# Row tiles over 64 slots with one product chunk a slot, shorter GpSimd chains, a second block's heads ahead of the steps, and no filler products

## The chip, the core and the metric

The kernel runs on one core of a Trainium2 chip. Its engines are TensorE (PE in the profile, its weight loads PEld), VectorE (DVE), ScalarE (ACT), GpSimd (POOL) and SyncE (SP), each with an instruction queue of its own, taken in order; they meet through semaphores. The metric is the device time of one execution in microseconds. Before the change the median of 3 runs is 1,875.82 us (1,875.80 to 1,886.55).

## The reference

Input x is 4 x 512 x 256 (batch B, time T, width D), cond is 4 x 256. Two layers follow each other, each added to its input. The first is a transformer block in the Poincare ball, all in fp32; the second is an LSTM with 256 units over the 512 time steps. Cut to what matters:

```
def plin(x, w, b): return expmap0(logmap0(x) @ w + b)      # the maps need the norm of each row
xm = expmap0(layer_norm(logmap0(x)) * (1 + sc_msa) + sh_msa)
q, k, v = heads(plin(xm, w_q, b_q)), ...                   # 16 heads of 16
out_h = expmap0(softmax(qt @ kt.T / 4) @ vt)               # each row attends to all 512
attn_out = plin(from_heads(out_h), w_o, b_o)
x = mobius_add(x, expmap0(g_msa * logmap0(attn_out)))
xm = expmap0(layer_norm(logmap0(x)) * (1 + sc_mlp) + sh_mlp)
ff = plin(plin(xm, w_f1, b_f1), w_f2, b_f2)                # 256 -> 1024 -> 256
x = mobius_add(x, expmap0(g_mlp * logmap0(ff)))            # then x = x_in + this
xW = x @ Wx + b                                            # LSTM, 512 steps, h0 = cond
def step(h, c, xw_t):
    a = xw_t + h @ Wh                                      # 4 x 1024
    i, f, o, g = sigmoid, sigmoid, sigmoid, tanh of its quarters
    c = f * c + i * g;  h = o * tanh(c)
```

A step needs the one before it. The block's rows need the attention of their block of 128 time positions, and row tile n (the 4 batches x 32 time positions 32n to 32n+31) must be through the block before step 32n can start.

## The kernel before

Up to about 254 us the kernel loads, normalizes x and computes q, k, v for 16 row groups, in loops. Then comes one sequence of slots, the same on all engines: slot g runs from FIRST (-126) to 511, and a slot g >= 0 contains step g of the LSTM. `pieces(g, ...)` adds what else stands in the slot, in this order:

- **Heads.** `attention(g)`: 256 heads of attention (4 blocks of 128 positions x 4 batches x 16 heads). `head_slot(n)` says where head n stands: block 0 in slots -126 to -63, one a slot; block 1 in slots 0 to 63; blocks 2 and 3 from slot 64 on, every second slot. A head is 4 score products on TensorE (L575), two exps of 128 x 512 on ScalarE, one in its slot and one in the next (L814, L808), a subtraction in two halves on VectorE (L1060) and, five slots later, 8 products with the values (L587).
- **Merges.** `merged(k, r)`: after 16 heads their norms are put right, over 9 slots, with 13 operations on GpSimd.
- **Row tiles.** `post(n, r)`: the 16 row tiles, each spread over PAUSE = 48 slots r, starting at slot 32n - 48, so that two tiles overlap by 16 slots. r = 0: product with w_o (L620) and its bias as a product (L622); r = 1 to 20: two GpSimd chains for the Moebius addition (`mobius_arg`, `mobius_factors`), then the norm and the scale (`to_ratio`, `to_norm`); r = 24 a transpose; r = 25 to 28 w_f1 (L637), two chunks a slot; r = 29 to 32 w_f2 (L645); r = 30, 31 the norm of the hidden row (L653); r = 34 to 40 Moebius again; r = 41 transpose (L659), r = 42 to 45 w_x, the input part of the gates (L669), two chunks a slot.
- **Output.** The 32 finished steps of a ring are transposed (L711), added and stored.

A *chunk* here is a set of fp32 products that streams 1,024 columns as the kernel's own planner counts them: two products of 128 columns, or one of 256, at four passes.

A **step** is on TensorE 32 products of 8 columns (L693) that add to gate inputs in PSUM; every 16 steps `put_round` loads the next 16 steps' inputs into PSUM first (L683). VectorE sums the halves (L1154, L1156, L1158), ScalarE takes tanh (L906, L908, L910), VectorE makes the cell (L1163), ScalarE its tanh (L912), and VectorE writes the new state in two fp16 halves (L1170, L1172), for which TensorE waits.

At the end of each slot `keep_busy` (L735) issues filler products of 256 columns into unused columns of a bank, onto zeros, until a slot has about 3,000 columns (3,600 where it has many of its own, 1,300 in the head slots ahead of the steps).

GpSimd's chains work on one number a row. In `Chain.link` every operation signals a semaphore and the engine waits for it before the next (L244 is a power, L292 and L294 belong to `clip`). Since each engine's queue is in order, a wait of one piece holds up the steps and heads that stand behind it. PSUM bank pM is shared, in an order that `PM_ORDER` computes and `wait_pM` enforces.

Of the kernel before, what the change touches and what calls it, by code (L numbers as in the profile page):

```python
# [43 lines left out]
class Chain:  # L44
# [23 lines left out]
FIRST = -126  # L68
PAUSE = 48
# [20 lines left out]
PM_READ = {"merged": "m_oc", "rows": "n_n1", "norm": "n_nfc", "out": "o_s"}  # L90
PM_ORDER = [use for slot, rank, use in sorted(
    [(merged_slot(k) + 8, 0, ("merged", k)) for k in range(NT)] +
    [(RING * n - PAUSE, 2, ("rows", n)) for n in range(NT)] +
    [(RING * n - PAUSE + 30, 1, ("norm", n)) for n in range(NT)] +
    [(RING * n + RING + 1, 3, ("out", n)) for n in range(NT)])]
# [17 lines left out]
def bass_hyperbolic_block_then_lstm(nc, x, cond, w_q, b_q, w_k, b_k, w_v, b_v, w_o, b_o, w_f1, b_f1, w_f2, b_f2,  # L113
                                    w_ada, b_ada, w_x, w_h, b_l, out):
    ctx = ExitStack()
    with ctx:
# [237 lines left out]
        def _(pool):  # L354
# [64 lines left out]
            def mobius_arg(ch, p, done):  # L419

                N = lambda name: one(name + p)
                clip(ch, N("s1"), N("n1"), 1, N("ca"), N("cb"))
# [4 lines left out]

            def mobius_factors(ch, p, nsq_x, done):

                N = lambda name: one(name + p)  # L430
# [4 lines left out]
                ch.link(g.tensor_tensor(N("cd"), N("cc"), N("y2"), ALU.add))
                ch.link(g.tensor_tensor(N("ca"), nsq_x, N("y2"), ALU.mult))
                ch.link(g.tensor_tensor(N("cb"), N("ca"), N("cc"), ALU.add))
                ch.link(g.tensor_scalar(N("ca"), N("cb"), EPS, None, ALU.max))
                power(ch, N("den"), N("ca"), DOWN, 1)
                ch.link(g.tensor_tensor(N("al"), N("cd"), N("den"), ALU.mult))  # L440
                ch.link(g.tensor_scalar(N("cb"), nsq_x, -1.0, 1.0, ALU.mult, ALU.add))
                ch.link(g.tensor_tensor(N("cc"), N("cb"), N("fac"), ALU.mult))
                g.tensor_tensor(N("be"), N("cc"), N("den"), ALU.mult).then_inc(s[done], 1)
# [775 lines left out]
```

## Time and profile before

| | before |
|---|---|
| median of 3 runs | 1,875.82 us |
| profiled execution | 1,876.28 us, span 1,874.4 us |
| mean granted clock | 0.858 |
| PE busy | 1,638.3 us (87%), 26,135 matmul records |
| DVE busy | 1,161.2 us (62%) |
| ACT busy | 936.6 us (50%) |
| POOL busy | 552.4 us (29%) |
| chain that ended last | PE 59%, POOL 11%, issue 7%, DVE 6%, ACT 3% |

Busy time is the union of an engine's records. PEclk is the TensorE clock that was granted: 1.0 is 2.4 GHz, 0.5 is 1.2 GHz. An fp32 product is split in the trace into two records. A row of a timeline gives the start in us, the time taken by the group, engine, line, operation, what it writes and reads, how many records it joins, and in brackets the idle time ahead of it and who ended it.

### The profile page before, as it was taken

To read this page: it belongs to the slowest core of one execution; us is meant where nothing else is said; L and a number is where in the kernel's file an instruction comes from. 1 tells how busy PE (TensorE), PEld (TensorE's weight loads), DVE (VectorE), ACT (ScalarE), POOL (GpSimd) and SP (SyncE) were. 2 spreads that over 40 slices of the span, in tenths; PEclk is the share of its full clock that TensorE was granted. 3 is DMA by queue.
4 is the path that set the end of the run, shared out by engine and by line. 5 is a ranking of instruction groups with operands and counts; after the bars stand their busy time and mean duration, and the time that the engine had idled before them with its cause. 6 is when DMAs were issued, how large, how long until landed. Compare 5 with 4: busy or idle time off the path is not lost.

```text
span 1874.4 us, 68150 instructions
## 1 busy us (share of the span) xinstructions
PE 1638.3 (87%) x26135; PEld 1394.2 (74%) x26135; DVE 1161.2 (62%) x6482; ACT 936.6 (50%) x3335; POOL 552.4 (29%) x1726
## 2 busy tenths in 40 slices
PE   3755589634999999999999999999999999999998
PEld 3544457423878888888787888888888888888887
DVE  6455555301677776767677777777766656666665
ACT  0334457412667565656565656565644544444443
POOL 4222212324042433333324242333333131413100
PEclk9676765555678689989899989898989999999999
DMA  7000000000000000000000000000000000000000
GB/s 225 0 0 0 0 1 1 1 0 3 2 3 8 3 9 3 9 3 9 3 9 3 9 5 6 9 3 8 3 8 3 9 2 8 5 3 6 3 6 5
DMA packets 16721, 18.53 MB, mean 10 GB/s; under 512 B 6036, under 2 KB 15384, under 8 KB 16408
## 3 DMA queue, kind: packets, MB, share of 16 engines
q1 hardware_dynamic: 13016, 10.51, 2.0%
q8 instruction: 201, 3.29, 0.7%
q10 hardware_dynamic: 3392, 3.81, 0.7%
q14 instruction: 112, 0.92, 0.2%
HBM read 12.21 MB, written 2.10 MB: 8 GB/s over the span
## 4 chain that ended last, share of the span: by engine, by line
PE 59%; POOL 11%; issue 7%; DVE 6%; ACT 3%; POOLq 1%; ACTq 0%; DVEq 0%
PE psum L735 19%; PE psum L693 17%; PE psum L669 5%; POOL sc L244 4%; PE psum L575 4%; PE psum L637 4%; PE psum L645 3%; PE psum L587 2%; PE psum L683 2%; PE psum L653 1%; DVE gA L1154 1%; PE psum L620 1%; DVE gF L1156 1%; DVE cnew L1163 1%; PE psum L622 1%
## 5 line engine op out<-in xcount | busy, mean ns | idle before, releaser
L735 PE MATMUL psum<-zeros,ident 128*128 128x256 f16 x4064 | 586.8, 290 | 19.8 <-DVE gF L1156 13.7
L693 PEld LDWEIGHTS psum<-hl,wh 128*128 128x128 f16 x16384 | 489.9, 97 | 75.7 <-DVE hl L1172 60.1
L693 PE MATMUL psum<-hl,wh 128*128 128x8 f16 x16384 | 516.4, 172 | 4.6 <-DVE hl L1172 3.3
L735 PEld LDWEIGHTS psum<-zeros,ident 128*128 128x128 f16 x4064 | 385.8, 103 | 113.1 <-DVE gF L1156 38.0
L906 ACT ACTIVATE tA<-gA 128x16 f32<-128x16 f32 x512 | 110.6, 216 | 523.9 <-DVE gA L1154 521.0
L1154 DVE TENSOR_REDUCE gA<-psum 128x16 f32<-128x32 f32 x512 | 96.8, 189 | 231.9 <-PE psum L693 228.9
L1060 DVE TENSOR_TENSOR weights<-w,weights 128x256 f16<-128x256 f32 x512 | 204.0, 419 | 38.5 <-ACT weights L808 38.4
L292 POOL TENSOR_SCALAR sc<-sc 128x1 f32<-128x1 f32 x97 | 23.5, 243 | 691.6 <-DVE sc L1131 299.6
L244 POOL TENSOR_TENSOR sc<-sc,cst 128x1 f32<-128x1 f32 (+1 forms) x260 | 198.3, 763 | 48.1 <-POOL sc L292 18.1
L808 ACT ACTIVATE weights<-psum 128x512 f16<-128x512 f32 x256 | 149.3, 583 | 22.1 <-PE psum L587 21.9
L814 ACT ACTIVATE w<-psum 128x512 f32<-128x512 f32 x256 | 149.9, 586 | 0.8 <-PE psum L575 0.7
L912 ACT ACTIVATE ot<-cnew 128x8 f32<-128x8 f32 x512 | 109.7, 214 | 80.5 <-DVE cnew L1163 24.5
L1170 DVE TENSOR_TENSOR hl<-ot 128x8 f16<-128x8 f32 x512 | 89.8, 175 | 93.0 <-ACT ot L912 92.0
L1163 DVE TENSOR_TENSOR_SCAN cnew<-cmul,cadd 128x24 f32<-128x24 f32 x512 | 107.2, 209 | 29.2 <-DVE cadd L1160 1.7
L575 PE MATMUL psum<-qTs,kT 64*128 64x128 f16 x1024 | 121.9, 252 | 2.5 <-issue 1.9
L1172 DVE TENSOR_TENSOR_SCAN hl<-ot,hl 128x24 f16<-128x24 f32 x512 | 106.6, 208 | 17.9 <-DVE hl L1170 0.2
L908 ACT ACTIVATE cmul<-gF 128x8 f32<-128x8 f32 x512 | 107.6, 210 | 0.0
L910 ACT ACTIVATE tO<-gO 128x8 f32<-128x8 f32 x512 | 105.9, 207 | 0.3
L669 PE MATMUL psum<-place,wx 128*128 128x128 f32 x512 | 99.1, 354 | 3.8 <-ACT arena L897 3.3
L1158 DVE TENSOR_REDUCE gO<-psum 128x8 f32<-128x16 f32 x512 | 88.9, 174 | 17.5
L587 PE MATMUL psum<-vs,weights 128*128 128x33 f16 x2048 | 96.4, 184 | 1.3 <-DVE weights L1060 0.8
L1156 DVE TENSOR_REDUCE gF<-psum 128x8 f32<-128x16 f32 x512 | 88.8, 173 | 8.7
(232 smaller groups left out, 2262.8 us busy)
## 6 DMA issues: line engine op xcount, KB each, us to landing
arena<-in_x_dram SPq DMA_DIRECT2D x4, 512.0 KB, 9.8
wf<-in_L_cond_w_f_dram SPq DMA_DIRECT2D x2, 1024.0 KB, 16.8
xr<-in_x_dram SPq DMA_DIRECT2D x64, 32.0 KB, 1.7
out_dram<-place SPq DMA_DIRECT2D x64, 32.0 KB, 1.6
qTs<-in_L_cond_w_ada_dram ACTq DMA_DIRECT2D x1, 1536.0 KB
oT<-in_L_cond_Wh_dram ACTq DMA_DIRECT2D x1, 1024.0 KB, 14.4
wx<-in_L_cond_Wx_dram SPq DMA_DIRECT2D x1, 1024.0 KB, 18.5
rows<-in_L_cond_b_ada_dram ACTq DMA_DIRECT2D x4, 128.0 KB, 14.2
```

Of the source, the lines that this page charges most:

```text
L244: ch.link(nc.gpsimd.tensor_tensor(dst, src, cst[:, which, 0:w], ALU.pow))
L575: last = mm(bank[m % 2][:, kc * P:(kc + 1) * P], kT[part, b, hp, kc * P:(kc + 1) * P], qTs[part, k, hp, :], start=True, stop=True, skip_gr ...
L587: last = mm(pV[:, h % 8 * W1:(h % 8 + 1) * W1], weights[:, m % 4, wl, kc * P:(kc + 1) * P], vs[:, k % B, kc, h, :], start=kc == 0 and wl = ...
L669: last = mm(pP[:, gi % 4 * P:(gi % 4 + 1) * P], wx[:, kc, c * P:(c + 1) * P], XT[:, kc, :], start=kc == 0, stop=kc == KD - 1, skip_group_c ...
L693: last = mm(cols, wh16[:, half, kc, (g0 + c) * P:(g0 + c + 1) * P], hl[:, :, kc, :, 2].rearrange("p e b -> p b e"), start=False, stop=c == ...
L735: mm(pF[:, D:2 * D], ident16[:], zeros[:], start=False, stop=False, skip_group_check=True)
L808: A(weights[:, m % 4, 0, :], bank[m % 2], ACT.Exp, scale=1.0 / (math.sqrt(HD) * QK_UP * QK_UP)).then_inc(s["t_e"], 1)
L814: A(w32[:, m % 4, :], bank[m % 2], ACT.Exp, scale=1.0 / (math.sqrt(HD) * QK_UP * QK_UP)).then_inc(s["t_E"], 1)
L906: A(tA[:], gA[:], ACT.Tanh, scale=down).then_inc(s["l_tA"], 1)
L1060: d.tensor_tensor(weights[:, m % 4, 1, part], w32[:, m % 4, part], weights[:, m % 4, 0, part], ALU.subtract).then_inc(s["t_l"], 1)
L1154: d.tensor_reduce(gA[:], gate_cols(0, i % ROUND), axis=AX.X, op=ALU.add).then_inc(s["l_gA"], 1)
L1163: d.tensor_tensor_scan(cnew[:].rearrange("p c e -> p (c e)"), cmul[:].rearrange("p c e -> p (c e)"), cadd[:].rearrange("p c e -> p (c e)") ...
```

## The change

- Row tiles take 64 slots instead of 48 (ROW_TILE), and start 65 slots ahead of their step (PAUSE): two tiles overlap by half. Each slot has one chunk of a tile where it had two: w_o in r = 1, 2, w_f1 in eight slots, w_f2 in six, w_x in seven (the last slot has two of its chunks). The bias b_o is added on VectorE instead of by a product.
- w_x uses bank pM, which now passes through one more use in `PM_ORDER`. Gate inputs are stored with time innermost.
- GpSimd's row chains are rewritten: operations with two scalars do the work of two, `Chain.send` issues an operation without waiting for it, and part of the series is computed while other engines work.
- Block 1's heads stand in slots -79 to -16; FIRST is -147. Blocks 2 and 3 start at slots 19 and 147, every second slot. A merge has 13 slots (SETTLE = 12).
- WANTED, EARLY and FIRST_STEPS are 0, and `keep_busy` issues nothing.

The diff, cut:

```diff
-FIRST = -126
-PAUSE = 48
+FIRST = -147
+PAUSE = 65
+ROW_TILE = 64
+SETTLE = 12
-LIGHT, HEAVY, EARLY = 3000, 3600, 1300
+WF1_AT = (26, 27, 28, 29, 30, 31, 33, 34)
+WF2_AT = (35, 36, 37, 42, 42, 43, 43, 44)
+GATES_AT = (57, 58, 59, 60, 61, 62, 63, 63)
+WANTED, EARLY, FIRST_STEPS = 0, 0, 0
-    return (FIRST + i, i, 64 + 2 * i, 192 + 2 * i)[block]
+    return (FIRST + i, FIRST + B * H + 4 + i, 19 + 2 * i, 147 + 2 * i)[block]
...
+    def send(self, ins):
+        self.n += 1
+        ins.then_inc(self.sem, 1)
...
+        def row_scale(ch, done):
+            g = nc.gpsimd
+            ch.send(g.tensor_scalar(one("la"), one("lE"), -2.0, one("z2"), ALU.mult, ALU.add))
+            ch.link(g.tensor_tensor(one("lb"), one("z1"), one("lE"), ALU.add))
+            power(ch, one("lc"), one("lb"), DOWN, 1)
+            ch.link(g.tensor_scalar(one("L1"), one("la"), one("lc"), one("ly"), ALU.mult, ALU.add))
...
-                    mm(pM[:, 0:D], ones[0:1, :], bo[0:1, :], start=False, stop=True, skip_group_check=True).then_inc(s["n_wo"], 1)
+                    d.tensor_tensor(vA, pM[:, 0:D], bo[:], ALU.add).then_inc(s["n_v"], 1)
...
+                for gi in range(GC):
+                    if r == GATES_AT[gi]:
+                        if gi == 0:
+                            pe.wait_ge(s["n_Xc"], n + 1)
+                            wait_pM("gates", n)
+                        else:
+                            pe.wait_ge(s["n_xc"], GC * n + gi)
...
-                wanted = LIGHT if cols < 2048 else HEAVY
-                if t < 0:
-                    wanted = EARLY if t in HEAD_AT else 0
-                count = max(0, -((cols - wanted) // D))
+                if t >= 0:
+                    count = int(min((WANTED - 256 - cols) / D, (1.2 - us) * 2400 / D))
+                    if t < 4:
+                        count = (FIRST_STEPS - 256 - cols) // D
+                else:
+                    count = (EARLY - cols) // D if t in HEAD_AT else 0
```

TensorE in the steps in which w_x's chunks stand, before (L693 is a step's products, L575 scores, L587 weighted values, L669 w_x, L735 fillers):

```order
L693 MATMUL psum<-hl,wh 128x8 x32
L575 MATMUL psum<-qTs,kT 128x128 x4
L669 MATMUL psum<-place,wx 128x128 x4
L735 MATMUL psum<-zeros,ident 128x256 x4
L693 MATMUL psum<-hl,wh 128x8 x32
L587 MATMUL psum<-vs,weights 128x33 x8
L669 MATMUL psum<-place,wx 128x128 x4
L735 MATMUL psum<-zeros,ident 128x256 x5
```

and with the change (L741 a step's products, L620 scores, L632 weighted values, L717 w_x, L685 w_f1 of the next tile):

```order
L741 MATMUL psum<-hl,wh 128x8 x32
L620 MATMUL psum<-qTs,kT 128x128 x4
L717 MATMUL psum<-place,wx 128x128 x2
L685 MATMUL psum<-uT,wf 128x128 x2
L741 MATMUL psum<-hl,wh 128x8 x32
L632 MATMUL psum<-vs,weights 128x33 x8
L717 MATMUL psum<-place,wx 128x128 x4
L685 MATMUL psum<-uT,wf 128x128 x2
```

A step has one chunk of either tile where it had two of one; the last such slot has three; the fillers are gone.

TensorE in the head slots ahead of the steps, before:

```order
L587 MATMUL psum<-vs,weights 128x33 x8
L575 MATMUL psum<-qTs,kT 128x128 x4
L735 MATMUL psum<-zeros,ident 128x256 x3
L587 MATMUL psum<-vs,weights 128x33 x8
L575 MATMUL psum<-qTs,kT 128x128 x4
```

and with the change:

```order
L620 MATMUL psum<-qTs,kT 128x128 x4
L632 MATMUL psum<-vs,weights 128x33 x8
L620 MATMUL psum<-qTs,kT 128x128 x4
L632 MATMUL psum<-vs,weights 128x33 x8
L620 MATMUL psum<-qTs,kT 128x128 x4
```

Only a head's own products are left; 128 heads stand there instead of 64.

GpSimd between the exp of the logarithm and the row scale. Before, the first ten of 29 operations:

```order
L465 TENSOR_TENSOR sc<-sc 128x1
L466 TENSOR_TENSOR sc<-sc 128x1
L244 TENSOR_TENSOR sc<-sc,cst 128x1
L468 TENSOR_TENSOR sc<-sc 128x1
L469 TENSOR_SCALAR sc<-sc 128x1
L470 TENSOR_TENSOR sc<-sc 128x1
L244 TENSOR_TENSOR sc<-sc,cst 128x1
L269 TENSOR_TENSOR sc<-sc 128x1
L270 TENSOR_SCALAR sc<-sc 128x1
L271 TENSOR_TENSOR sc<-sc 128x1
```

and with the change all of them (L256 is a power):

```order
L341 TENSOR_SCALAR sc<-sc 128x1
L342 TENSOR_TENSOR sc<-sc 128x1
L256 TENSOR_TENSOR sc<-sc,cst 128x1
L344 TENSOR_SCALAR sc<-sc 128x1
L345 TENSOR_SCALAR sc<-sc 128x1
L346 TENSOR_TENSOR sc<-sc 128x1
L347 TENSOR_SCALAR sc<-sc 128x1
L348 TENSOR_TENSOR sc<-sc 128x1
L349 TENSOR_SCALAR sc<-sc 128x1
L256 TENSOR_TENSOR sc<-sc,cst 128x1
L351 TENSOR_TENSOR sc<-sc 128x1
```

Eleven are left in this place; ten that need no exp stand ahead of it (L328 to L336).

## Rows read from the trace of the kernel before

**Rows 1.** Page, part 2: granted clock in 40 slices of 46.9 us.
```profile
PEclk9676765555678689989899989898989999999999
```
**Rows 2.** Page, part 5: the fillers; busy us, mean ns, idle before, releaser.
```profile
L735 PE MATMUL psum<-zeros,ident 128*128 128x256 f16 x4064 | 586.8, 290 | 19.8 <-DVE gF L1156 13.7
```
**Rows 3.** Windows, second sum of a step alone: stretch, us, busy (count), PEclk, DMA, GB/s.
```profile
461.80:673.80 212.00, 11.07 (x64) 0.74 0.01 4
673.80:1384.00 710.20, 44.33 (x256) 0.95 0.02 6
1384.00:1757.40 373.40, 25.03 (x144) 0.99 0.02 6
1757.40:1870.00 112.60, 8.38 (x48) 1.00 0.02 4
```
**Rows 4.** Windows of all engines: PE, PEld, DVE, ACT, POOL busy, PEclk, DMA, GB/s.
```profile
276.00:288.00 12.00, 12.00 (x121) 8.69 (x120) 6.51 (x18) 8.91 (x16) 0.21 (x1) 0.50 0.01 1
...
636.00:640.00 4.00, 4.00 (x62) 3.10 (x58) 2.65 (x16) 2.32 (x10) 2.31 (x11) 0.50 0.00 0
```
**Rows 5.** Timeline of a step at granted clock 0.50.
```profile
656.62 1.05 PE L693 MATMUL psum<-hl,wh 128*128 128x8 f16 x32
...
657.27 0.19 DVE L1154 TENSOR_REDUCE gA<-psum 128x16 f32<-128x32 f32 x1 [0.80 <-PE psum L693]
...
657.52 0.39 PE L587 MATMUL psum<-vs,weights 128*128 128x33 f16 x8
...
657.84 0.60 PE L575 MATMUL psum<-qTs,kT 64*128 64x128 f16 x4
...
658.37 2.07 PE L669 MATMUL psum<-place,wx 128*128 128x128 f32 x8
...
658.99 0.76 DVE L1060 TENSOR_TENSOR weights<-w,weights 128x256 f16<-128x256 f32 x2
...
660.24 0.85 PE L735 MATMUL psum<-zeros,ident 128*128 128x256 f16 x3
660.48 0.91 ACT L897 ACTIVATE arena<-psum,blc,unit 128x128 f32<-128x128 f32 x2 [1.05 <-PE psum L669]
...
660.88 0.59 PE L693 MATMUL psum<-hl,wh 128*128 128x8 f16 x15
```
**Rows 6.** Timeline of a step in the tail, granted clock 1.00.
```profile
1841.76 0.21 DVE L1172 TENSOR_TENSOR_SCAN hl<-ot,hl 128x24 f16<-128x24 f32 x1
...
1842.03 1.01 PE L693 MATMUL psum<-hl,wh 128*128 128x8 f16 x32
1842.64 0.19 DVE L1154 TENSOR_REDUCE gA<-psum 128x16 f32<-128x32 f32 x1 [0.53 <-PE psum L693]
```
**Rows 7.** Timeline: ScalarE's exps of heads ahead of the steps.
```profile
273.83 0.60 ACT L808 ACTIVATE weights<-psum 128x512 f16<-128x512 f32 x1 [0.38 <-PE psum L587]
...
274.37 0.60 ACT L814 ACTIVATE w<-psum 128x512 f32<-128x512 f32 x1
...
275.35 0.60 ACT L808 ACTIVATE weights<-psum 128x512 f16<-128x512 f32 x1 [0.38 <-PE psum L587]
```
**Rows 8.** Timeline: TensorE and VectorE wait for a row tile's X.
```profile
544.17 0.48 DVE L1146 SCALAR_TENSOR_TENSOR X<-X,sc,xr 128x256 f32<-128x256 f32 x1 [1.21 <-POOL sc L443]
...
545.23 0.69 PE L659 MATMUL psum<-ident,X 128*128 128x128 f32 x2 [1.23 <-DVE X L1148]
```
**Rows 9.** Timeline: first and last of 29 operations of GpSimd's long chain.
```profile
388.14 0.19 POOL L465 TENSOR_TENSOR sc<-sc 128x1 f32<-128x1 f32 x1 [0.42 <-ACT sc L854]
...
399.96 0.24 POOL L287 TENSOR_SCALAR sc<-mv 128x1 f32<-128x1 f32 x1 [0.20 <-POOL sc L286]
```
**Rows 10.** Timeline: tile 0's first product, step 0's products, the last step's second sum.
```profile
367.04 0.77 PE L620 MATMUL psum<-wo,oT 128*128 128x256 f32 x1 [0.56 <-ACT oT L828]
...
461.02 1.05 PE L693 MATMUL psum<-hl,wh 128*128 128x8 f16 x32
...
1868.53 0.18 DVE L1156 TENSOR_REDUCE gF<-psum 128x8 f32<-128x16 f32 x1
```

More of the change, by code:

```diff
@@ L89 @@
 HEAD_AT = {head_slot(n): n for n in range(HEADS)}
-PM_READ = {"merged": "m_oc", "rows": "n_n1", "norm": "n_nfc", "out": "o_s"}
+PM_READ = {"merged": ("m_oc", 1), "rows": ("n_v", 1), "norm": ("n_nfc", 1), "gates": ("n_xc", GC), "out": ("o_s", 1)}
 PM_ORDER = [use for slot, rank, use in sorted(
[L92 to L95, printed above, removed]
+    [(merged_slot(k) + SETTLE, 0, ("merged", k)) for k in range(NT)] +
+    [(RING * n - PAUSE + 1, 2, ("rows", n)) for n in range(NT)] +
+    [(RING * n - PAUSE + 38, 1, ("norm", n)) for n in range(NT)] +
+    [(RING * n - PAUSE + 57, 1, ("gates", n)) for n in range(NT)] +
+    [(RING * n + RING + 4, 3, ("out", n)) for n in range(NT)])]
 def pieces(g, attention, merged, post, out):
@@ new lines, in row_series @@
+        def row_series(ch):
+            g = nc.gpsimd
+            ch.send(g.tensor_scalar(one("z2"), one("z1"), 2.0, None, ALU.mult))
+            ch.send(g.tensor_tensor(one("ndi"), one("nd1"), cst[:, DOWN, 0:1], ALU.pow))
+            ch.send(g.tensor_scalar(one("negm"), mv1[:, 0:1], -1.0, None, ALU.mult))
+            ch.send(g.tensor_copy(one("varn"), mv1[:, 1:2]))
+            ch.link(g.tensor_tensor(one("nn"), one("nc1"), one("nc1"), ALU.mult))
+            ch.send(g.tensor_scalar(one("small"), one("nn"), SERIES_BELOW, None, ALU.is_lt))
+            ch.link(g.tensor_scalar(one("ser"), one("nn"), 1.0 / 9, 1.0 / 7, ALU.mult, ALU.add))
+            for term in (1.0 / 5, 1.0 / 3, 1.0):
+                ch.link(g.tensor_scalar(one("ser"), one("ser"), one("nn"), term, ALU.mult, ALU.add))
@@ L435, in mobius_factors @@
[L435 to L441, printed above, removed]
@@ L602, in wait_pM @@
                     kind, i = PM_ORDER[before]
-                    pe.wait_ge(s[PM_READ[kind]], i + 1)
+                    read, each = PM_READ[kind]
+                    pe.wait_ge(s[read], each * (i + 1))
             def merged(k, r):
-                if r == 8:
+                if r == SETTLE:
                     pe.wait_ge(s["m_oS"], k + 1)
@@ L629, in post @@
                     last.then_inc(s["n_uT"], 1)
[L630 to L631 removed]
+                if r in WF1_AT:
+                    c = WF1_AT.index(r)
                     pe.wait_ge(s["n_uc"], n + 1)
[L633 to L639 removed]
@@ new lines, in post @@
+                    for kc in range(KD):
+                        last = mm(pP[:, c % 4 * P:(c % 4 + 1) * P], wf1[:, kc, c * P:(c + 1) * P], uT[:, 0, kc, :],
+                                  start=kc == 0, stop=kc == KD - 1, skip_group_check=True)
+                    last.then_inc(s["n_f"], 1)
+                for kc in range(KF):
+                    if r == WF2_AT[kc]:
+                        if kc == 0:
+                            pe.wait_ge(s["n_fc"], KF * n + KF)
+                        last = mm(pP[:, 0:D], fT[:, kc, :], wf2[:, kc, :], start=kc == 0, stop=kc == KF - 1, skip_group_check=True)
+                        if kc == KF - 1:
+                            last.then_inc(s["n_f2"], 1)
```

275 lines of the change are left out of this document (146 added, 129 removed).

## The prediction

> **What bounds the kernel now.** I read the page first. TensorE is busy nearly everywhere, but 587 us of its time are the filler products of L735 [rows 2], so its share says little; the clock it was granted is between 0.5 and 0.7 in much of the first 600 us and near 1.0 later [rows 1]. The count of steps by stretch is more telling: 64 steps in 212 us (3.31 us each), then 256 in 710 us (2.77), 144 in 373 us (2.59), and the last 48 in about 2.33 us each [rows 3]. A step is a loop through three engines: products, sums on VectorE, four tanh on ScalarE, the new state on VectorE, products. In the tail, at the upper clock level (2.4 GHz, granted 1.0), the first sum begins 0.61 us after the first product, and the second half of the state (L1172) begins 0.27 us ahead of the next product; the loop takes 2.33 us there [rows 6]. All that a step takes beyond that is TensorE's other work, or a wait.
>
> Two kinds of excess stand out. Where the clock is granted 0.50 (the lower level, 1.2 GHz [rows 4]), a step with a whole head, two chunks (four fp32 products of 128 columns, which the trace shows as eight records) and three fillers takes 4.26 us (656.62 to 660.88 [rows 5]); nearly all of it is TensorE streaming. And once per row tile TensorE waits for GpSimd's chain of one-column operations: at 545.23 us it had been idle 1.23 us for X, which VectorE could write only after GpSimd [rows 8]. Ahead of step 0 the kernel spends 208 us, from the first head (254 us) to the first step's sum at 461.7 us.
>
> **Prices at the lower clock.** Everything that follows depends on whether TensorE's clock rises without fillers. In the head slots ahead of the steps it ran without a gap for 12 us at a time, with three fillers to a head, and stayed at 0.50; in steps with eight fillers it was at 0.50 too [rows 4]. The change takes away every filler, and its heaviest step streams less than those stretches did. I take 0.50 for the whole recurrence.
>
> The loop itself loses little by that. At 0.50 the 32 products of a step take 1.05 us against 1.01, and the first sum comes 0.65 us after the first product against 0.61 [rows 5, 6]. So a bare step is 2.33 + 0.05 = **2.38 us**. Its bounds are 2.33 (nothing is lost) and 3.31, the mean of the 64 first steps, most of them at 0.50 [rows 3]; I stay near the lower one, since those carried fillers and heads.
>
> Other work starts 0.90 us after the first product (656.62 to 657.52). From start to start [rows 5]: weighted values of a head 0.32, scores 0.53, two chunks (2,048 columns) 1.87. One chunk alone is then 0.94, and I take 1.02, as it changes operands once for half as many columns. A step exceeds 2.38 only if 0.90 plus these does.
>
> **The steps after the change.** Per 32 steps there are 26 chunks (2 for w_o, 8 each for w_f1, w_f2 and w_x), two loads of a round of gates (2,048 columns each) and a few transposes. Two tiles overlap by 32 slots, so chunks pair up: nine steps have two, one has three. With the two rounds that is eleven steps with 1.87 us of large products. With heads, odd steps have scores and even ones weighted values:
> - seven with scores: 0.90 + 0.53 + 1.87 = 3.30, 0.92 over;
> - four with weighted values: 3.09, 0.71 over; together 9.3 us;
> - the triple step 0.90 + 0.32 + 2.73 = 3.95, and 0.64 more because the two w_x chunks of slot 63 stand in one slot and the second waits for ScalarE's copy of the first (0.46 for one of two copies that take 0.91 [rows 5], and 0.18 of handover): 2.2 over;
> - single chunks with a transpose or scores: 1.2 in all;
> - VectorE: its free time in a step is 0.53 us [rows 6]; half a head takes about 0.4 of it (0.76 for two halves) and a row operation 0.48 more [rows 5, 8], so some ten steps that TensorE doesn't stretch are 0.3 to 0.5 longer: 3.7.
>
> Sum 16.4 us per 32 steps. Heads fill steps 19 to 278, 8.1 such rounds: 133 us. Without heads the eleven are 0.39 over, the triple 1.9: 6.3 us per 32, times 6.2: 39 us. The first 19 steps add 2 and the end 0.4. With 512 x 2.38 = 1,219 that makes **1,393 us** between the first and the last sum; before it is 1,406.6 (461.9 to 1,868.5, by the sums of rows 3 and 10). The change gains **13 us** here: it loses about 25 us on bare steps and in the stretches that were at 1.0, wins back some 30 in the first 64 steps, which lose their fillers and one of two exps, and the rest from waits that go.
>
> **GpSimd's chain.** What it removes is real. One row tile's long chain took 29 operations and 12.1 us (388.14 to 400.20 [rows 9]), 0.37 to 0.42 us for a linked operation and 0.75 for a power. Now eleven operations follow the exp (4.7 us by these prices); ten of the rest stand ahead of it, most without waiting for each other. A tile's five chains go from about 35 us to 27. In 64 slots of 2.4 us each stage has one or two slots of its own, so I expect no wait of TensorE for them in the recurrence, and I cost the merge of heads at nothing there: GpSimd is idle over half of each round.
>
> **Ahead of step 0.** Here the slots are short and the cover is gone. One head costs ScalarE two exps 0.54 us apart; TensorE's three fillers made it 1.52 from one to the next [rows 7], now about 1.09. 64 more heads are moved here. Tile 0 may start after 78 heads: 254.4 + 2 + 78 x 1.09 + 3.2 for four merges = 345 us, against 367.0 [rows 10]. Its first 25 slots took 37 us; the chains save 7, a merge on GpSimd now stands in their way (13 of its operations, 9, from the prices above and a wider power), waits of ScalarE and VectorE for results that come later than a 1.09 us slot allows give 2: 41, so 386. Slots 26 to 43 each stream heads and a chunk, 1.87 us mostly: 35, so 421. Then GpSimd has two tiles' chains and a merge in a row: 26, so 447; the eight w_x chunks paired with w_f1's, 14 with their start; the round 1.8. The first product comes at about 463 us, against 461.0: **2 us lost**. Bounds: 445, if the chains hide behind heads, and 480, if each slot's waits add up.
>
> **The sum.** The profiled execution took 1,876.3 us with a span of 1,874.4; the median of the runs is 1,875.8, half a microsecond below. 1,876.3 + 2 - 13.6 = 1,864.7, less 0.5: **1,864 us**.
>
> **Rivals.**
> 1. *The clock stays up.* For it: after the change a bare step leaves TensorE idle only about 1 us at a time. Then a bare step is 2.33, paired chunks fit (0.90 + 0.27 + 0.94 = 2.11), and only the triple step and VectorE's excess are left, 6.3 us a round with heads and 0.8 without: 1,249 us for the steps, 1,720 in all. Against it: 12 us without a gap at 0.50 [rows 4]. 4%. The Trainium skill, "TensorE: Matmul & The Clock Gate", in its table "Why this matters for your kernels", asks only that no long idle gap stand between bursts. By that rule this rival would be the forecast; the gap-free rows at 0.50 show that it isn't enough here.
> 2. *It rises where chunks pair up*, seven slots in a row. The eleven steps lose most of their excess: 61 us with heads, 27 without, 1,776 in all. For it: in the first 64 steps, where two chunks stand in a step, it did rise, to a mean of 0.74 [rows 3]. Against it: those had fillers too. 8%.
> 3. *The part ahead of the steps shrinks*, the chains hiding behind heads: 445, so 1,846. 18%.
> 4. *Slower: the copies reach the tanh.* A chunk now ends with the step, and ScalarE's copy (0.46) starts with the next products; the first tanh follows 0.88 us after them (0.65, and a sum of 0.19 with its handover). By my prices 0.3 us is left. If waking, a second copy and VectorE's row operations together put the tanh 0.2 us late in the 16 to 20 chunk steps, that is 3 to 4 us a round, 50 us over 14 rounds, 1,914 in all; it decides from 0.06 us over all 512 steps, which makes 1,895. For it: at 660.48 ScalarE's copy is still running when the next products start [rows 5]. 22%.
>
> **The numbers.** The forecast's own case has 48% and reaches from 1,845 to 1,888. The range that holds 8 in 10 is 1,825 to 1,905: it leaves out rivals 1 and 2 (12%) and the upper part of rival 4. A measurement of this kernel tells 1% from no change, 19 us: below 1,857 is faster, above 1,895 slower. Faster: 4 + 8 + 16 of rival 3 + 10 of the forecast's case = 38%. Slower: 20 of rival 4 and 2 of the forecast = 22%. The same: 40%.
>
> **What would show it.** The granted clock in the steps: 0.5 nearly throughout, else rival 1 or 2. The last 30 steps: 2.38 us each (2.33 to 2.42). The stretch of steps 64 to 255: about 2.89 us a step; 320 to 463: 2.58. Paired chunks from start to start: 1.87. No wait of TensorE on X or on the normalized rows. First product of step 0 at 445 to 480 us. It is wrong if bare steps exceed 2.45 us, or if a step waits for ScalarE's copies.

## The result, and the profile after

The changed kernel takes **1,778.96 us** (median of 4 runs, 1,772.66 to 1,785.78); before, 4 runs beside them gave 1,875.81. The ratio is 0.9476 (95% interval 0.943 to 0.9522): 5% faster, where 1,864 us had been forecast, with a range that began at 1,825. Ratios leave out executions over 1.5% above the fastest of their kernel and medians keep them, which is why e1 and e4 below look slower by median than by ratio. The profiled execution took 1,775.52 us, its span is 1,773.8 us and its mean granted clock 0.599, against 0.858 before. Times after this are of profiled executions where a single step is spoken of, and ratios of runs where kernels are compared.

The page of the changed kernel: busy time by engine, the granted clock in 40 slices of 44.3 us (it answers to [rows 1]), and the chain of waits by engine.

```profile
PE 1325.2 (75%) x22039; PEld 1125.0 (63%) x22039; DVE 1168.5 (66%) x6498; ACT 940.3 (53%) x3335; POOL 520.5 (29%) x1438
...
PEclk9676765555656565656566665556565565656555
...
PE 49%; DVE 17%; ACT 5%; issue 4%; POOL 2%; DVEq 0%; POOLq 0%
```

The clock is granted at half in much of the recurrence, as forecast, but many slices show 0.6. The second sum of a step alone, by stretch (stretch, us, busy time and count, granted clock, DMA share, GB/s), which answers to [rows 3]:

```profile
474.00:638.70 164.70, 11.17 (x64) 0.61 0.02 4
638.70:1303.00 664.30, 44.68 (x256) 0.59 0.02 6
1303.00:1655.60 352.60, 25.25 (x144) 0.58 0.02 5
1655.60:1768.50 112.90, 8.41 (x48) 0.50 0.01 3
```

The count gives the time of a step: 2.57, 2.59, 2.45 and 2.35 us, where [rows 3] have 3.31, 2.77, 2.59 and 2.35. From the first second sum (474.08) to the last (1,767.67) it is 1,293.6 us, against 1,406.6 before and 1,393 in the forecast. Ahead of step 0 the kernel takes 12 us longer (474.1 against 461.9). So the forecast missed the steps by 99 us, and the part ahead by 10 the other way.

**A bare step.** Timeline in the tail, where nothing stands beside a step (start, us, engine, line, operation, records, idle time ahead and its releaser), and the windows of all engines there, below it:

```profile
1740.94 0.21 DVE L1236 TENSOR_TENSOR_SCAN hl<-ot,hl 128x24 f16<-128x24 f32 x1
...
1741.20 1.02 PE L741 MATMUL psum<-hl,wh 128*128 128x8 f16 x32 [1.31 <-DVE hl L1236]
1741.84 0.19 DVE L1218 TENSOR_REDUCE gA<-psum 128x16 f32<-128x32 f32 x1 [0.55 <-PE psum L741]
...
1743.54 1.02 PE L741 MATMUL psum<-hl,wh 128*128 128x8 f16 x32 [1.31 <-DVE hl L1236]
```
```profile
1700.00:1712.00 12.00, 5.62 (x162) 4.87 (x162) 7.98 (x53) 4.38 (x22) 0.00 (x0) 0.50 0.05 13
```

At granted 0.50 the state is 0.26 us ahead of the products and the first sum 0.64 us after them; from products to products it is 2.34 us, and the median of the bare steps of the whole trace is 2.33. The loop of [rows 6], at 1.00, takes 2.32 (1,842.03 to 1,844.35): about 0.01 us is lost at the lower clock, and 0.05 was forecast.

**Paired chunks.** TensorE and windows of all engines around slot 63 of one ring of 32 slots:

```profile
701.39 0.61 PE L620 MATMUL psum<-qTs,kT 64*128 64x128 f16 x4
701.92 1.22 PE L717 MATMUL psum<-place,wx 128*128 128x128 f32 x4
702.94 1.06 PE L685 MATMUL psum<-uT,wf 128*128 128x128 f32 x4
703.79 1.04 PE L741 MATMUL psum<-hl,wh 128*128 128x8 f16 x32
...
719.26 0.71 PE L717 MATMUL psum<-place,wx 128*128 128x128 f32 x4 [0.55 <-ACT arena L951]
719.81 0.61 PE L685 MATMUL psum<-uT,wf 128*128 128x128 f32 x4
720.26 1.00 PE L741 MATMUL psum<-hl,wh 128*128 128x8 f16 x32
...
724.89 1.01 PE L741 MATMUL psum<-hl,wh 128*128 128x8 f16 x32
725.83 0.39 PE L620 MATMUL psum<-qTs,kT 64*128 64x128 f16 x4
726.15 0.71 PE L685 MATMUL psum<-uT,wf 128*128 128x128 f32 x4
726.70 0.60 PE L667 MATMUL psum<-wo,oT 128*128 128x256 f32 x2
727.20 1.01 PE L741 MATMUL psum<-hl,wh 128*128 128x8 f16 x32
```
```profile
702.00:716.00 14.00, 14.00 (x190) 13.32 (x191) 8.58 (x53) 9.37 (x31) 6.10 (x12) 0.50 0.01 2
716.00:730.00 14.00, 12.74 (x246) 10.96 (x245) 9.56 (x58) 9.76 (x36) 0.00 (x0) 0.91 0.01 3
```

Two chunks take 1.87 us from start to start (701.92 to 703.79), exactly as priced, and TensorE has no pause in these 14 us. Then the granted clock goes to the upper level: at 726.15 a chunk takes 0.55 from start to start, two 1.05, and the step with two chunks and scores takes 2.31 us in place of 3.38. At 719.26 stands the wait of slot 63 for ScalarE's copy, priced at 0.64 with a handover; it is 0.55 to 0.94 over the 15 tiles.

In all, 128 steps have two chunks. Beside heads (steps 19 to 278) 25 of 72 ran in under 2.5 us, elsewhere 23 of 56; of the 31 loads of a round, 8 did. At the lower clock the steps with two chunks take 3.38 with scores, 2.97 with weighted values and 2.75 with neither.

**VectorE.** A step with half a head's low weights (L1112) and a row operation (L1156):

```profile
727.20 0.42 DVE L1112 TENSOR_TENSOR weights<-w,weights 128x256 f16<-128x256 f32 x1
727.53 0.42 DVE L1156 TENSOR_TENSOR place<-psum,bo 128x256 f32<-128x256 f32 x1
727.87 0.18 DVE L1218 TENSOR_REDUCE gA<-psum 128x16 f32<-128x32 f32 x1
```

The operations are 0.42 us long but start 0.33 and 0.34 apart. The sum starts 0.67 us after the products (727.20), 0.06 later than in [rows 6] at the same clock, and the step still takes 2.32 us.

**GpSimd and X.** TensorE's waits from 474 us on: X and the normalized rows are gone from them. A line gives who waited for whom, the total in us, how often, and the longest.

```profile
PE psum L741 <- DVE hl L1236: 259.0, 307, 1.5
PE psum L717 <- ACT arena L951: 10.5, 15, 0.9
```

Ahead of step 0 the wait on X stands once (it answers to [rows 8]), behind GpSimd's queue of two tiles and a merge; the last row answers to [rows 10]:

```profile
351.23 1.22 PE L667 MATMUL psum<-wo,oT 128*128 128x256 f32 x2
...
395.96 0.69 PE L677 MATMUL psum<-ident,place 128*128 128x128 f32 x2 [0.58 <-ACT place L918]
...
459.02 0.69 PE L706 MATMUL psum<-ident,X 128*128 128x128 f32 x2 [7.90 <-DVE X L1212]
```

### The profile page after: what moved, and what is told of

The parts are those of the page before. It is cut to its first block, busy times and chain, and to the rows that moved or that the text cites. A ratio compares the mean times of both kernels' runs of the same rounds, so it can differ in the third digit from the quotient of the medians.

```text
span 1773.8 us, 59205 instructions
## 1 busy us (share of the span) xinstructions
PE 1325.2 (75%) x22039; PEld 1125.0 (63%) x22039; DVE 1168.5 (66%) x6498; ACT 940.3 (53%) x3335; POOL 520.5 (29%) x1438
## 3 DMA queue, kind: packets, MB, share of 16 engines
q8 instruction: 169, 2.77, 0.7%
## 4 chain that ended last, share of the span: by engine, by line
PE 49%; DVE 17%; ACT 5%; issue 4%; POOL 2%; DVEq 0%; POOLq 0%
PE psum L741 27%; PE psum L717 5%; PE psum L692 4%; DVE cnew L1227 4%; ACT ot L964 4%; PE psum L685 4%; DVE hl L1236 4%; DVE hl L1234 3%; DVE gO L1222 3%; PE psum L731 3%; PE psum L620 2%; DVE cadd L1224 2%; PE psum L700 1%; PE psum L667 1%; PE psum L632 1%
## 5 line engine op out<-in xcount | busy, mean ns | idle before, releaser
L741 PEld LDWEIGHTS psum<-hl,wh 128*128 128x128 f16 x16384 | 496.7, 103 | 352.9 <-DVE hl L1236 331.7
L741 PE MATMUL psum<-hl,wh 128*128 128x8 f16 x16384 | 524.0, 172 | 259.8 <-DVE hl L1236 259.0
L958 ACT ACTIVATE tA<-gA 128x16 f32<-128x16 f32 x512 | 110.4, 216 | 465.5 <-DVE gA L1218 465.5
L1112 DVE TENSOR_TENSOR weights<-w,weights 128x256 f16<-128x256 f32 x512 | 202.8, 419 | 35.2 <-ACT weights L861 34.2
L867 ACT ACTIVATE w<-psum 128x512 f32<-128x512 f32 x256 | 156.2, 610 | 24.7 <-DVE weights L1112 22.8
L620 PE MATMUL psum<-qTs,kT 64*128 64x128 f16 x1024 | 146.6, 293 | 16.8 <-ACT weights L861 13.8
L256 POOL TENSOR_TENSOR sc<-sc,cst 128x1 f32<-128x1 f32 (+1 forms) x180 | 148.2, 823 | 33.8 <-POOL sc L304 12.2
L717 PE MATMUL psum<-place,wx 128*128 128x128 f32 x512 | 128.4, 393 | 11.6 <-ACT arena L951 11.0
L632 PE MATMUL psum<-vs,weights 128*128 128x33 f16 x2048 | 101.6, 191 | 38.9 <-DVE weights L1112 29.5
L692 PE MATMUL psum<-wf,arena 128*128 128x256 f32 x256 | 128.3, 626 | 0.0
L632 PEld LDWEIGHTS psum<-vs,weights 128*128 128x128 f16 x2048 | 80.8, 107 | 63.0 <-DVE weights L1112 54.9
L685 PE MATMUL psum<-uT,wf 128*128 128x128 f32 x512 | 113.3, 361 | 0.0
L717 PEld LDWEIGHTS psum<-place,wx 128*128 128x128 f32 x512 | 98.2, 270 | 20.2 <-ACT arena L951 14.9
```

The source lines that it names most:

```text
L620: last = mm(bank[m % 2][:, kc * P:(kc + 1) * P], kT[part, b, hp, kc * P:(kc + 1) * P], qTs[part, k, hp, :], start=True, stop=True, skip_gr ...
L632: last = mm(pV[:, h % 8 * W1:(h % 8 + 1) * W1], weights[:, m % 4, wl, kc * P:(kc + 1) * P], vs[:, k % B, kc, h, :], start=kc == 0 and wl = ...
L685: last = mm(pP[:, c % 4 * P:(c % 4 + 1) * P], wf1[:, kc, c * P:(c + 1) * P], uT[:, 0, kc, :], start=kc == 0, stop=kc == KD - 1, skip_group ...
L692: last = mm(pP[:, 0:D], fT[:, kc, :], wf2[:, kc, :], start=kc == 0, stop=kc == KF - 1, skip_group_check=True)
L717: last = mm(pM[:, gi % 4 * P:(gi % 4 + 1) * P], wx[:, kc, c * P:(c + 1) * P], XT[:, kc, :], start=kc == 0, stop=kc == KD - 1, skip_group_c ...
L741: last = mm(cols, wh16[:, half, kc, (g0 + c) * P:(g0 + c + 1) * P], hl[:, :, kc, :, 2].rearrange("p e b -> p b e"), start=False, stop=c == ...
```

## The experiments

Each ran in three timed rounds beside the kernel before, except e6, which ran once. A kernel's time is also given as its ratio to that kernel. The sums are the second sum of a step, read from each trace as above. The edits shown are cut to what matters; a time given for phase p of a ring of 32 is the time up to the second sum of step 32k + p.

| run | ratio (95%) | median, us | first sum at | first to last sum |
|---|---|---|---|---|
| before | 1 | 1,875.8 | 461.9 | 1,406.6 |
| changed | 0.9476 (0.943 to 0.9522) | 1,779.0 | 474.1 | 1,293.6 |
| e1 changed, fillers | 0.9459 (0.9404 to 0.9514) | 1,793.0 | 472.9 | 1,293.8 |
| e2 before, no fillers | 1.0365 (1.0301 to 1.0429) | 1,944.5 | 444.3 | 1,486.5 |
| e3 = e2, heads ahead | 1.0398 (1.0354 to 1.0442) | 1,951.6 | 482.3 | 1,460.5 |
| e11 = e2, short chains | 1.0096 (1.0066 to 1.0126) | 1,898.7 | 430.4 | 1,456.1 |
| e4 changed, old chains | 0.9654 (0.9588 to 0.972) | 1,828.7 | 486.5 | 1,312.5 |
| e5 changed, capped fillers | 0.9508 (0.9437 to 0.9579) | 1,780.3 | 472.9 | 1,290.2 |
| e7 changed, w_f1 doubled | 0.9557 (0.9521 to 0.9592) | 1,798.3 | 474.3 | 1,318.6 |
| e8 changed, heads in steps | 0.9521 (0.9484 to 0.9559) | 1,790.5 | 438.1 | 1,344.5 |
| e9 changed, w_f2 single | 0.9362 (0.9335 to 0.9389) | 1,760.0 | 474.8 | 1,268.7 |
| e10 = e9, no triples | 0.937 (0.9343 to 0.9397) | 1,764.9 | 473.5 | 1,287.8 |
| e12 = e9, fillers ahead of pairs | 0.9509 (0.9478 to 0.9539) | 1,788.9 | 474.0 | 1,309.4 |

### What each part of the change is worth (e2, e3, e11, e4)

```diff
# e2, on the kernel before
-LIGHT, HEAVY, EARLY = 3000, 3600, 1300
+LIGHT, HEAVY, EARLY = 0, 0, 0
# e3, on e2
-FIRST = -126
+FIRST = -147
-    return (FIRST + i, i, 64 + 2 * i, 192 + 2 * i)[block]
+    return (FIRST + i, FIRST + B * H + 4 + i, 19 + 2 * i, 147 + 2 * i)[block]
```

> The kernel before, with no fillers and nothing else changed. Theory A: the 64 head slots fall from 1.52 to 1.09 us (27 us less) and the first 64 steps from 3.3 to about 2.6 (45 less), but the steps with two chunks of one tile, 12 in 32, go from 2.6 to 3.4 at the lower level (some 70 to 100 more over all tiles), and the waits for GpSimd stay: 1,850 to 1,900 us, so fillers alone decide little. Theory B (the gain of the change is the fillers' removal and the rest moves nothing): 1,800 us or less.

> The kernel before, with no fillers, and with block 1's heads ahead of the steps and blocks 2 and 3 at the slots of the change. Theory A: 64 heads leave steps that had room for most of them and cost 1.1 us each ahead of the steps, partly beside tile 0's chain on GpSimd: 15 to 45 us more than the same kernel with the heads in the steps. Theory B (two exps a step are what stretched the first steps): the same or less.

e11 puts the changed kernel's `mobius_arg`, `mobius_factors`, `row_ratio`, `row_series` and `row_scale` into e2; e4 puts the old ones into the changed kernel.

> The kernel before with no fillers and the short chains on GpSimd (the argument, the factors and the row numbers as in the changed kernel), its 48-slot tiles, two chunks a slot and heads as they were. Without fillers it took 1,944 us. Theory (the longer chains delayed the row tiles by waits on X of 5.1 us and more, as old chains in the changed kernel cost 50 us): 1,890 to 1,920, and waits for X below 3 us. Rival (in 48 slots TensorE's own stacks of up to four chunks set the time): 1,930 to 1,945, which would leave the whole of the rest to the spread slots.

> The changed kernel with the GpSimd chains of before (every operation waited for, 29 operations behind the exp). Theory A: the long chain takes 12 us where the slots from 17 to 20 leave 7, so VectorE and then TensorE wait some 3 to 5 us in each of 15 tiles, and the part ahead of the steps grows by 10 to 25: 1,830 to 1,870 us. Theory B (64 slots alone give the chains the room they need): within 1% of the changed kernel plus the part ahead, 1,800 us or less.

Without fillers the kernel before is 3.65% slower, outside both of e2's bands. Ahead of step 0 it gains 18 us (three fillers a head stood in the way there), and its steps lose 80; the first 64, expected 45 us shorter, took 216 us in place of 212. The heads ahead bring no gain in that layout: 38 us more ahead, 26 less in the steps, 7 us more in all, less than e3's theory had and within the noise. The short chains bring 2.7% there, as e11's theory had it. TensorE's waits in e2, and the same of e11 with no such line left:

```profile
PE psum L693 <- DVE hl L1172: 338.9, 313, 1.9
PE psum L659 <- DVE X L1148: 21.9, 14, 2.2
PE psum L669 <- ACT arena L897: 3.9, 15, 0.3
```
```profile
PE psum L733 <- DVE hl L1212: 336.4, 311, 1.9
PE psum L709 <- ACT arena L937: 3.9, 15, 0.3
```

In the changed kernel the old chains cost 1.8% by the ratios, more than e4's theory B allowed and, at 1,828.7 us, just under theory A's band. In its trace the steps of phase 20 take 4.0 to 4.8 us, because VectorE waits for the row scale (2.01 us at 1,131.71).

By the ratios: fillers off +3.7%, short chains -2.7%, heads ahead +0.3%, and what then remains between e11 with heads ahead and the changed kernel is **-6.5%, 122 us**: 64-slot tiles with one chunk of a tile in a slot, the bias on VectorE, w_x in bank pM and merges of 13 slots. That is a remainder: it takes the heads' share from another pair of runs than the chains', and no run has the 64-slot tiles alone. The traces agree with it in kind. In e11 the steps exceed 2.33 us by 265 us in all, 131 of them in steps of over 3.5 us, where up to four chunks or a load of a round stand together; in the changed kernel it is 103 and 18.

### Is it the even spread? (e7, e9, e10)

```diff
# e7
-WF1_AT = (26, 27, 28, 29, 30, 31, 33, 34)
+WF1_AT = (26, 26, 28, 28, 30, 30, 33, 33)
# e9: and what follows w_f2 on VectorE and ScalarE 2 slots later, X in slot 55 as before
-WF2_AT = (35, 36, 37, 42, 42, 43, 43, 44)
+WF2_AT = (35, 36, 37, 42, 43, 44, 45, 46)
# e10, and what follows w_f2 another slot later on VectorE and ScalarE
+WF1_AT = (26, 27, 28, 29, 30, 33, 34, 35)
+WF2_AT = (36, 37, 42, 43, 44, 45, 46, 47)
```

> The changed kernel with the chunks of the first feed-forward product two to a slot (26, 28, 30 and 33) in place of one a slot; all other work stands where it stood. Four times a ring two steps of two chunks become one of three and one of one. Theory (a step pays only what stands above its free time, so work that is evened out is cheaper): 2 x 2.75 us become 3.7 + 2.35, +0.5 each at the lower clock and +0.1 at the upper, 64 times: 1,787 to 1,811 us. Rival (the sum of the work counts, not its place): 1,774 to 1,784.

> The changed kernel with the chunks of the second feed-forward product one a slot also at 42 to 46 (before two each at 42 and 43), so that the two steps of two chunks at phase 10 and 11 are gone; what follows on VectorE and ScalarE comes two slots later, the argument and factors on GpSimd at 50 and 52, X in slot 55 as before. Theory (a step pays what stands above its free time; a pair cost 1.05 and 0.64 beside heads, 0.42 and 0.42 without, nearly all at the lower clock): 8 x 1.6 + 8 x 0.8 = 19 us less, time 1,757 to 1,764 us, steps of phase 10 and 11 at 2.33 to 2.55. Rival 1 (the steps of two chunks are what brings the upper clock, and without these it is up in fewer of the later ones): 1,765 to 1,779. Rival 2 (X comes too late and the steps wait at phase 23 and 24): 1,785 or more.

> As the run with chunks one a slot at 42 to 46, and the chunk of the first product that made three in slot 31 moved to 35, so that the second product stands in 36, 37 and 42 to 47. Theory: the triples (4.07 beside heads, 3.23 without) become pairs of at most 3.4 and 2.9, another 5 to 8 us less: 1,750 to 1,758 us. Rival (the double slot 63 waits for its copy whatever stands beside it): as the run before it, 1,757 to 1,764; second rival (X late): above 1,780.

e7 came out in the expected band: three chunks take 4.23 us beside a head and 3.60 without at the lower clock, one 2.32 to 2.33, against two steps of 3.38 and 2.97, or of 2.75. TensorE in e7, from one step's products to the next:

```profile
706.16 1.04 PE L742 MATMUL psum<-hl,wh 128*128 128x8 f16 x32
...
708.69 1.91 PE L686 MATMUL psum<-uT,wf 128*128 128x128 f32 x8
...
710.39 1.04 PE L742 MATMUL psum<-hl,wh 128*128 128x8 f16 x32
```

The place of the work counts, not its sum. e9 is the mirror: the steps of phase 10 and 11 fell from 3.38 and 2.97 to 2.53 and 2.45 (2.33 without heads), and the kernel to 1,760.0 us. It also moved the clock, and rival 1 had that the other way round. Windows of all engines, e9, over one stretch of five paired steps:

```profile
697.00:703.00 6.00, 6.00 (x90) 5.72 (x87) 3.72 (x23) 4.20 (x14) 3.23 (x4) 0.56 0.01 3
703.00:714.00 11.00, 9.94 (x189) 9.07 (x187) 7.51 (x46) 8.23 (x29) 3.25 (x9) 0.93 0.02 4
```

Here the clock rises after two paired steps, and phases 28 to 30 take 2.32; so it is, to 0.1 us, in seven of the eight rings beside heads, while in the changed kernel it is in three, and in four it rises only behind phase 30. So 32 of e9's 56 paired steps beside heads were under 2.5 us, and 23 of the same 56 in the changed kernel. e10 turns the triples into pairs (4.0 to 3.5 us beside heads), and gives it all back: 14 of those 56 were under 2.5, and its rounds none of 16. It is no faster than e9 and misses its theory's band.

### What raises the clock? (e1, e5, e12)

```diff
# e1
+WANTED, EARLY, FIRST_STEPS = 3000, 0, 3000
# e5
+                    count = int((1.1 - us - cols / 2400) * 1200 / D)
# e12, on e9
+                    count = int((1.2 - us) * 2400 / D) if (t + 1) % RING in (21, 22, 23, 24, 25) else 0
```

> The changed kernel with its own filler planner switched on (3,000 columns a step, limited to the time a step has free; none ahead of the steps). Theory A (a bare step costs 2.33 us at either clock level, and what the lower level costs is only the steps with two or three chunks): the paired steps fall from 3.38 and 2.97 to about 2.4 us, bare steps stay at 2.33, some 65 to 80 of the 100 us that the changed kernel spends above 2.33 a step go, 1,700 to 1,725 us. Theory B (fillers stand in the way of the state's products, as in the first 64 steps before): the steps with fillers are longer than 2.33, and the time is 1,760 us or more.

> The changed kernel with filler products of 256 columns that are counted at their duration at the lower clock (0.213 us each) and so fit the free time of the step at either clock: 5 in a bare step, fewer beside a head, none where two chunks stand, none ahead of step 0. Theory (the clock had risen by itself in part of the paired stretches, and steady work would hold it): bare steps stay at 2.33, paired steps fall to 2.32 and rounds to 2.5, granted clock above 0.7, time 1,725 to 1,755 us. Rival (what a filler gives at the upper clock it takes at the lower, as in the run with full fillers, where 1,774 to 1,807 was measured): 1,770 to 1,790, and some bare steps over 2.4. Second rival (the clock does not answer to them): 1,779, with the granted clock below 0.62.

> The version with chunks one a slot at 42 to 46 (1,760 us), and filler products only in the five slots of phase 21 to 25 of each ring, ahead of the five steps of two chunks: up to 11 in a slot, counted at their duration at the upper clock (0.107 us), none elsewhere. Without them the granted clock is at the lower level in these slots and in the first two paired steps (3.38 and 2.9 beside heads, 2.75 without), and at the upper in the next three. Theory (TensorE without pause raises the clock whatever it computes, and the rise only comes earlier): the paired steps start at 2.32, 1.7 us less a ring with heads and 0.85 without, against 0.9 for every filler slot that is still at the lower clock (two or three of them): 1,755 to 1,775 us. Rival (fillers do not raise it, as those counted at the lower clock did not): five slots at about 3.2 in each ring, 60 us more, 1,800 to 1,830.

e1 holds a mean clock of 0.775 and gains nothing, as theory B had it. e5 fits its fillers in: bare steps stay at 2.33, and the clock stays where it was (0.605), which is the second rival. Windows of all engines: e1 in 38 us with fillers at the lower clock, and after them; e5 over one ring; e12 over the filler slots of one ring and over the paired steps behind them.

```profile
1399.50:1437.90 38.40, 37.84 (x506) 29.71 (x502) 20.47 (x132) 11.39 (x57) 15.03 (x49) 0.50 0.01 2
1453.00:1465.00 12.00, 10.95 (x198) 9.54 (x198) 6.90 (x48) 6.94 (x29) 0.00 (x0) 1.00 0.01 1
```
```profile
1200.00:1280.00 80.00, 75.93 (x1227) 60.24 (x1226) 53.07 (x344) 38.69 (x169) 27.04 (x80) 0.56 0.02 6
```
```profile
1427.10:1437.30 10.20, 10.03 (x133) 7.71 (x131) 5.52 (x33) 2.85 (x14) 3.57 (x10) 0.50 0.01 2
1437.30:1453.50 16.20, 14.52 (x289) 12.95 (x287) 10.20 (x70) 10.13 (x42) 0.00 (x0) 0.98 0.01 3
```

In e1 TensorE was busy for 37.84 of 38.40 us at granted 0.50, and each step took 3.2 us, because ten fillers don't fit at that clock. In this ring of e12 it rose after three filler steps of 3.4 us, and the paired steps then took 2.31 to 2.32. The fillers cost 3 x 1.1 us there and won 0.7: in e9 the clock rises in the same five steps without them (2.72, 2.35, 2.48, 2.42 and 2.31). Over the whole trace the filler slots add 44 us to e9's. That is between the theory (it does rise earlier) and the rival (it costs more than it brings); the time, 1,788.9 us, is in neither band. What decides when the clock rises remains open: it rose after two paired steps (e9), after three with eleven fillers each (e12), and not in the twelve of e1's window, most of them with ten. The Trainium skill, "TensorE: Matmul & The Clock Gate", in its table "Why this matters for your kernels", promises the full clock to a TensorE that is kept busy without a break, in a row that the forecast left out when it wrote "only"; the row of e1 does not agree with it, nor do the 14.00 busy of 14.00 us at 0.50 in the changed kernel.

### VectorE's price (e6, one run)

```diff
+EXTRA = {15: 3, 17: 1, 18: 1, 19: 2}      # phase: additional products of 256 columns, in steps 64 to 255
```

> The changed kernel with additional VectorE products of 256 columns, used by nothing, behind the half of the low weights in steps 64 to 255: one in the slots of phase 17 and 18 of each ring of 32, two in phase 19, three in phase 15; these steps carry a head and no chunk. The forecast priced one such operation in a step at about 0.3 us. Theory from the trace of the changed kernel (operations of the queue start 0.33 apart and one fits the idle time of VectorE): one adds 0.00 to 0.05, two add 0.3 to 0.5, three 0.6 to 0.9 to the step. By the forecast's price: 0.3, 0.7 and 1.1. Sum over six rings by the theory: 6 to 9 us; by the forecast's price 14.

The run took 1,778.5 us. One operation added 0.00 us (2.33 and 2.34 in phases 17 and 18, as without it), two 0.27 (2.61 against 2.34), three 0.60 (2.97 against 2.37). Step with two:

```profile
684.96 0.41 DVE L1116 TENSOR_TENSOR weights<-w,weights 128x256 f16<-128x256 f32 x1
685.30 0.75 DVE L1127 TENSOR_TENSOR junk<-rows 128x256 f16<-128x256 f32 x2
685.97 0.18 DVE L1228 TENSOR_REDUCE gA<-psum 128x16 f32<-128x32 f32 x1
```

The theory holds for one; two came in under its band, three at its lower end. The step after three was 2.94 in place of 3.38: its round load had started while VectorE was still late, so part of the 0.60 came back.

### The heads ahead of step 0 (e8)

```diff
-    return (FIRST + i, FIRST + B * H + 4 + i, 19 + 2 * i, 147 + 2 * i)[block]
+    return (FIRST + i, -18 + i, 47 + 2 * i, 175 + 2 * i)[block]
```

> The changed kernel with the heads of the second block in slots -18 to 45 in place of -79 to -16 (the third and fourth block follow 28 slots later, every second slot as before). Theory (the heads ahead of step 0 are what makes its part longer than forecast; in the kernel before without fillers they moved the first sum from 444 to 482): first sum of gates at 440 to 455 in place of 474, and steps 0 to 45, which now carry a head each, 0.1 to 0.3 us longer: 1,750 to 1,770 us. Rival (the chain of tile 0 through VectorE and GpSimd sets the first product whatever stands beside it): first sum 468 to 478, steps longer, 1,780 to 1,795 us.

The theory's cause was right (first sum at 438, 36 us earlier) and its total wrong: the steps lost 51 us. The time lies in the rival's band, whose cause (first sum unmoved) was wrong. Some 21 us of the 51 are a collision: blocks later by 28 slots put a merge into GpSimd's queue just ahead of a row tile's clip. Timeline, e8:

```profile
607.45 0.25 POOL L306 TENSOR_SCALAR sc<-sc 128x1 f32<-128x1 f32 x1 [0.20 <-POOL sc L256]
607.73 0.51 ACT L918 ACTIVATE place<-place,sc 128x256 f32<-128x256 f32 x1 [2.54 <-POOL sc L306]
...
608.14 0.20 ACT L958 ACTIVATE tA<-gA 128x16 f32<-128x16 f32 x1
```

ScalarE waited 2.54 us with the step's tanh (L958) queued behind it, so this step took 4.5 to 4.9 us in place of 2.55, in each of ten rings. Without that, some 30 us lost would stand against 36 won: by this account, which no run shows alone, it hardly matters where the second block's heads stand.

## Why the prediction was wrong

**Bare step, 2.33 + 0.05: failed.** It is 2.33 at granted 0.50, 0.01 above the loop at 1.00. The 0.65 of [rows 5] was read from a step with a head and fillers (0.63 to 0.64 in a bare one), and 0.05 was charged to all 512: 26 us too much, and 2 more because 511 steps, not 512, lie between the first and the last sum. The upper bound stood on "most of" the first 64 steps being at 0.50; [rows 3] give them a mean of 0.74.

**VectorE, 3.7 us per 32 steps: failed.** Beside heads the steps in question exceed 2.33 by about 5 us in all, not 30; 3 of them lie in one step of a ring (phase 23, three large operations behind the low weights, 0.4 each). The forecast laid 0.48 and 0.4 end to end into 0.53 of free time; queued operations start 0.33 apart, and e6 shows that one more costs nothing. About 25 us too much.

**Clock of 0.50 throughout: failed, though it was read from gap-free rows.** The prices of paired steps at 0.50 were right (3.30 and 3.09 forecast, 3.38 and 2.97 measured; two chunks 1.87). But 48 of 128 paired steps ran in under 2.5 us, and the paired steps and rounds exceed 2.33 by 70.6 us in place of 102: 32 us too much. The triples exceed it by 21 in place of 30, the single chunks by about 5 in place of 10. With the other two these make the 99. The 102 was itself a little low: at the measured prices of the lower clock throughout, the paired steps and rounds would exceed 2.33 by about 110 us (an estimate), so the clock's rises were worth some 40.

**Rival 2** named this last mechanism and came to 1,776 us; but it is only a third of the miss, so that its time agrees is mostly chance. It took all paired steps as won, and kept the two terms above. Its 8% was too little, but not for the row given in its favour, a mean clock of 0.74 in the first 64 steps [rows 3]: in the same layout without fillers those steps are at 0.50, as the forecast argued. Window of all engines, e2, its first 64 steps:

```profile
444.00:660.00 216.00, 182.06 (x3029) 154.11 (x3026) 144.35 (x819) 132.04 (x463) 69.16 (x220) 0.50 0.01 4
```

The error was to conclude from gap-free rows at 0.50 [rows 4] that no stretch of the changed kernel would rise.

**Steps 64 to 255 at 2.89, 320 to 463 at 2.58, tail at 2.38**: 2.62, 2.45, 2.35.

**GpSimd's chains cause no wait of TensorE in the recurrence: right.** Their worth was not in the sum by itself; it is 1.8% in this layout (e4), where the old chains do make VectorE, and TensorE behind it, wait in phase 20.

**Ahead of step 0, 463: the mechanism right, the size 10 us short, within its bounds of 445 to 480.** Its own stations were w_o at 345, row transpose at 386, X's transpose at 447, first products at 463; measured 351.2, 396.0, 459.0, 473.3. Six of the ten were lost before w_o. A head takes 0.98 us there, less than the 1.09 taken, but each merge stops the heads for 3 us or more, where the sum had 0.8:

```profile
326.91 0.27 POOL L468 TENSOR_SCALAR sc<-sc 128x16 f32<-128x16 f32 x1 [0.50 <-POOL sc L467]
327.21 0.43 DVE L1147 TENSOR_TENSOR oS<-uo,sc 128x256 f32<-128x256 f32 x1 [4.25 <-POOL sc L468]
327.56 1.09 DVE L1112 TENSOR_TENSOR weights<-w,weights 128x256 f16<-128x256 f32 x3
...
328.07 0.60 ACT L867 ACTIVATE w<-psum 128x512 f32<-128x512 f32 x1 [2.91 <-DVE weights L1112]
```

VectorE waits for GpSimd's merge with the low weights (L1112) queued behind it, and the next exp waits for those. The rest is spread over the stations behind it, among them a wait of TensorE of 7.9 us for X. The heads moved there are what costs (36 us in e8, 38 in e3), which the sum did hold.

**Rival 4, copies that reach the tanh**, did not happen: the 42 steps with one chunk and no head take 2.34 us on average, and paired steps are as long as TensorE's products make them at the lower clock (14.00 of 14.00 us busy).

## What to carry to other kernels

In a recurrence with a fixed loop time, work beside it is free up to the free time of the step and is paid in full above that: spread it one piece a step before making any piece faster (e7 against the changed kernel and e9, 1,798, 1,779 and 1,760 us). Take the price of a small operation from a place where it stands alone in the step that is to be forecast: 0.05 us from a crowded step, times 512, and durations laid end to end on a queue whose starts overlap, made half of this error. Whether fillers pay depends on the layout: the kernel before loses 3.65% without them (e2), and the changed kernel, whose steps mostly fit at the lower clock, gains nothing by them (e1, e5).

## What the runs showed of the hardware

- 32 products of 8 columns with their weight loads take 1.02 to 1.04 us at granted 0.50 (1,741.20 and 703.79) and 1.00 to 1.01 at the upper level (720.26, 724.89). What the clock changes is the wide products: two chunks take 1.87 us against 1.05.
- TensorE can be busy for 37.84 of 38.40 us with the granted clock at 0.50 throughout (e1).
- The clock's response depends on where the busy steps stand: with two pairs fewer per ring it rose after two paired steps in seven of eight rings beside heads (e9), with the triples evened out as well, in fewer (14 of 56 paired steps under 2.5 us in place of 32, e10). A version that evens out TensorE's work further can so be no faster.
- In the trace of the changed kernel a power of one column takes 0.57 us on GpSimd (324.85), one of 16 columns 2.93 (461.67, L256), so a merge fills GpSimd's queue for longer than its 13 operations suggest.
